# First FFN layer: weight rounding and squares moved to ScalarE, and the order of tile 0 changed

## What is computed

```python
def _quant_weight(w):
    gamma = jnp.mean(jnp.abs(w)) + EPS
    wq = jnp.clip(jnp.round(w / gamma), -1.0, 1.0) * gamma
    return w + jax.lax.stop_gradient(wq - w)
def _quant_act(x):
    scale = Q_MAX / jnp.clip(jnp.max(jnp.abs(x), axis=-1, keepdims=True), EPS)
    xq = jnp.clip(jnp.round(x * scale), -Q_MAX - 1.0, Q_MAX) / scale
    return x + jax.lax.stop_gradient(xq - x)
def bitlinear(x, w):
    return jnp.einsum('bsi,oi->bso', _quant_act(x), _quant_weight(w))
h = bitlinear(x, w1)
h = jnp.square(jax.nn.relu(h))
return bitlinear(h, w2)
```

## Time and profile before

| | us |
|---|---|
| median of 3 runs | 1647.94 (1645.99 to 1648.37) |
| the profiled execution | 1649.19 |
| its span, first to last instruction | 1647.9 |
| busy: PE, DVE, ACT, POOL | 1518.6, 1232.9, 888.3, 690.4 |
| share of the span: PE, DVE, ACT, POOL | 92%, 75%, 54%, 42% |
| mean granted TensorE clock | 0.975 |

### The profile page before, as it was taken

How to read it: one execution, slowest core, us unless ns; L and a number is a source line. 1 busy time by engine, 2 the same in 40 slices (tenths; PEclk the granted TensorE clock), 3 DMA queues, 4 the chain that set the end, 5 groups by cost and what they waited for, 6 DMA issues and landing times.

```text
span 1647.9 us, 26508 instructions
## 1 busy us (share of the span) xinstructions
PE 1518.6 (92%) x8800; PEld 1188.3 (72%) x8842; DVE 1232.9 (75%) x3031; ACT 888.3 (54%) x2404; POOL 690.4 (42%) x832
## 2 busy tenths in 40 slices
PE   4899999999999999999998789999986799999987
PEld 4778888888888888888886556666655576666653
DVE  4777776777777767767778867777787878888774
ACT  3666665666656656566666233333323366666655
POOL 2445555465555546455555000000004455555443
PEclk8999999999999999999998899999999799999999
DMA  6011111111110111111345666666655001111000
GB/s 263 14 42 62 40 65 39 39 65 48 50 58 39 65 40 52 52 49 54 123 174 191 223 221 207 219 210 216 219 194 182 14 20 52 46 52 40 26 14 26
DMA packets 50823, 156.71 MB, mean 95 GB/s; under 512 B 5888, under 2 KB 6016, under 8 KB 49280
## 3 DMA queue, kind: packets, MB, share of 16 engines
q1 hardware_dynamic: 50688, 155.02, 26.5%
HBM read 113.05 MB, written 41.94 MB: 94 GB/s over the span
## 4 chain that ended last, share of the span: by engine, by line
PE 66%; DVE 21%; ACT 5%; issue 5%; DMA 1%; POOL 1%; SPq 0%; DVEq 0%; ACTq 0%; POOLq 0%
PE bank L287 10%; PE bank L317 9%; PE bank L370 9%; PE bank L1140 8%; PE quad L357 5%; PE bank L1194 3%; PE quad L1169 3%; PE quad L345 3%; PE quad L347 3%; PE quad L346 3%; DVE bh L2015 2%; DVE wk L1971 2%; PE bank L329 2%; PE quad L1670 2%; PE bank L1578 2%
## 5 line engine op out<-in xcount | busy, mean ns | idle before, releaser
L535 ACT ACTIVATE Pt<-Pt,small 128x384 f32<-128x384 f32 (+1 forms) x256 | 172.8, 682 | 118.7 <-DVE small L754 118.5
L317 PE MATMUL bank<-wq,xT 128*128 128x512 f32 x768 | 207.1, 405 | 3.9 <-DVE wq L649 3.3
L370 PE MATMUL bank<-PT,vv 128*128 128x512 f32 x672 | 201.2, 408 | 9.2 <-DVE PT L739 5.4
L961 POOL TENSOR_SCALAR Pt<-Pt,small 128x384 f32<-128x384 f32 (+1 forms) x256 | 162.5, 648 | 86.9 <-DVE small L762 86.7
L754 DVE CUSTOM_DVE_ANT_0 Pt<-quad,mask,small 128x384 f32<-128x384 f32 (+1 forms) x256 | 171.2, 679 | 28.2 <-PE quad L347 26.8
L1140 PE MATMUL bank<-wq,ot 128*128 128x512 f32 x768 | 190.1, 400 | 1.6 <-DVE xr L1286 0.8
L739 DVE TENSOR_TENSOR PT<-quad,PT 128x512 fp32r<-128x512 f32 x224 | 153.7, 686 | 40.4 <-ACT PT L527 39.7
L1140 PEld LDWEIGHTS bank<-wq,ot 128*128 128x128 f32 x768 | 143.2, 190 | 34.2 <-issue 3.6
L317 PEld LDWEIGHTS bank<-wq,xT 128*128 128x128 f32 x768 | 137.9, 190 | 30.7 <-DVE wq L649 4.6
L949 POOL TENSOR_TENSOR t<-t 128x512 f32<-128x512 f32 x64 | 84.0, 1313 | 151.4 <-DVE t L720 151.4
L370 PEld LDWEIGHTS bank<-PT,vv 128*128 128x128 f32 x672 | 117.7, 191 | 32.7 <-DVE PT L739 13.7
(11 more groups left out here) (269 smaller groups left out, 3533.5 us busy)
## 6 DMA issues: line engine op xcount, KB each, us to landing
ot_scratch<-OT SPq DMA_DIRECT2D x64, 512.0 KB, 2.7
ot<-ot_scratch SPq DMA_DIRECT2D x64, 512.0 KB, 3.8
wkv_f<-in_w SPq DMA_DIRECT2D x12, 512.0 KB, 5.6
wkc_f<-in_w SPq DMA_DIRECT2D x12, 512.0 KB, 6.7
wkv_f<-in_wg SPq DMA_DIRECT2D x11, 512.0 KB, 4.7
wkv_f<-in_wd SPq DMA_DIRECT2D x11, 512.0 KB, 5.3
wkv_f<-in_wu SPq DMA_DIRECT2D x10, 512.0 KB, 4.7
stg<-in_ctxT SPq DMA_DIRECT2D x16, 256.0 KB, 3.3
```

The source lines that it names most:

```text
L317: ins = pe.matmul(bQ[:], xT[p][:, k, qt * 128:qt * 128 + 128], wq[j][:, g, k, :], start=(part == 0 and k == 0), stop=(part == 2 and k == 3))
L370: ins = pe.matmul(bO[:], vv[x][:, bg % 2, kt, :], PT[y][:, k % 2, :], start=(kt == 0 and n == 0), stop=(kt == tiles_in(i) - 1 and n == 2))
L535: act.activation(p, p, ACT.Exp, bias=nm[:, i % 2, h:h + 1], scale=-1.0, accum_out=sm[:, i % 2, h:h + 1]).then_inc(f["s_exp"], 1)
L961: pool.tensor_scalar(p, p, ri[:, i % 2, h:h + 1], 1.0, ALU.mult, ALU.mult).then_inc(f["p_n"], 1)
```

## The change

Four things are changed, all in the first FFN layer.

1. Ternary chunks: w1's last two, w2's last six and the second layer's T steps of tiles up to 13 are no longer compared by DVE. ACT multiplies the raw chunk by 1/gamma and adds 12582912 in f32, which rounds to whole numbers, in place (`act_levels`, first pass); a second pass subtracts it and writes bf16; DVE clips to -1 and +1 (`dve_clip`). The new semaphore t_lev counts the passes, and the raw buffer is free behind the second. `dve_gamma` and `dve_l_scale` work out one reciprocal more.
2. Squares: ACT squares each half of the relu in place with the scale inside the operation (`act_square`); DVE only rounds. The chain of small operations for the scale takes a maximum with the root of the bound and one operation less stands ahead of the scale.
3. Order: `pe_w2_sum` and `dve_gamma(1)` come ahead of group 3 of tile 0; w2's last two chunks come behind the squares on ACT; the loads of steps 0 to 2 come ahead of the ot loads 13 and 14, and ACT takes these three magnitudes at the end of tile 0 and not in tile 1.
4. The load of rope signals on the semaphore of the constants, and waits for the first use of these.

```diff
+WHOLE = 12582912.0
...
-        sp.dma_start(rope[:], a["rope"]).then_inc(f["tables_in"], 16)
+        sp.wait_ge(f["consts"], 1)
+        sp.dma_start(rope[:], a["rope"]).then_inc(f["const"], 16)
...
+    both = [k for k in range(ends[NT - 2]) if seq[k][0] == "T"]
...
+            elif k - 3 in both:
+                sp.wait_ge(f["t_lev"], 2 * (mem["shared"] + done[k - 3]))
...
             sp_ot(4 * n + 12)
+            if n < NT - 2:
+                sp_w(range(3) if n == 0 else range(ends[n + 1], ends[n + 2]))
             if n == 0:
                 sp_ot(13)
                 sp_ot(14)
-            if n < NT - 2:
-                sp_w(range(3) if n == 0 else range(ends[n + 1], ends[n + 2]))
...
+        pe_w2_sum()
         pe_y(0, 3)
-        pe_w2_sum()
         pe_y(1, 0)
...
+    def act_l(k):
+
+        if seq[k][0] == "A":
+            act_l_abs(k)
+        else:
+            w = seq[k][1]
+            act.wait_ge(f[f"g_w{k % 3}"], 16 * (k // 3 + 1))
+            act.wait_ge(f["w_gamma"], 2 * (2 + w) + 2)
+            mem["act_levels"](chunk(k), wraw[k % 3], gam1[:, w, 4:5], mem["shared"] + both.index(k))
+
+    def act_w2(q):
+        act.wait_ge(f[f"f_in{(0, 1, 3, 6)[q // 2]}"], (96, 96, 32, 32)[q // 2])
+        mem["act_ternary"](1, q)
+
+    def act_square(n, j):
+        s = slice(j * 1024, j * 1024 + 1024)
+        act.wait_ge(f["u_max"], 5 * n + 5)
+        act.wait_ge(f["relu"], 6 * n + 2 * j + 2)
+        act.activation(r_[:, s], r_[:, s], ACT.Square, scale=cl[:, n % 2, 22:23]).then_inc(f["relu"], 1)
...
     def act_program():
+        act.wait_ge(f["w_gamma"], 2)
+        mem["act_ternary"](0, 6)
+        mem["act_ternary"](0, 7)
+        act.wait_ge(f["w_gamma"], 4)
+        act_w2(2)
         for n in range(NT):
             act_xq(n)
+            if n == 0:
+                act_w2(3)
+                act_w2(4)
+                act_w2(5)
...
-            if n == 1:
-                act_l_abs(0)
-                act_l_abs(1)
+            for j in range(2):
+                act_square(n, j)
+            if n == 0:
+                act_w2(6)
+                act_w2(7)
             for j in range(2):
                 act_hT(n, j)
-            for k in visits(n, "A")[2 if n == 1 else 0:]:
-                act_l_abs(k)
+            if n < NT - 2:
+                for k in range(3) if n == 0 else range(max(ends[n], 3), ends[n + 1]):
+                    act_l(k)
...
+            dve.reciprocal(gm[:, 4:5], gm[:, 0:1]).then_inc(f["w_gamma"], 1)
...
         v.settle()
-        v.did(dve.scalar_tensor_tensor(c[:, 19:20], c[:, 17:18], c[:, 17:18], eps, ALU.mult, ALU.max))
-        v.settle()
-        v.did(dve.reciprocal(c[:, 20:21], c[:, 19:20]))
-        v.settle()
-        v.did(dve.tensor_tensor(c[:, 22:23], c[:, 20:21], c[:, 21:22], ALU.mult))
+        v.did(dve.tensor_scalar(c[:, 18:19], c[:, 17:18], float(1e-5 ** 0.5), None, ALU.max))
+        v.settle()
+        v.did(dve.reciprocal(c[:, 20:21], c[:, 18:19]))
+        v.settle()
+        dve.tensor_scalar(c[:, 22:23], c[:, 20:21], float(127 ** 0.5), c[:, 16:17],
+                          ALU.mult, ALU.mult).then_inc(f["u_max"], 1)
+        v.did(dve.tensor_tensor(c[:, 19:20], c[:, 18:19], c[:, 18:19], ALU.mult))
+        v.settle()
         v.did(dve.tensor_scalar(c[:, 23:24], c[:, 19:20], 1.0 / 127, gam[:, 1, 0:1], ALU.mult, ALU.mult))
...
-        dve.wait_ge(f["relu"], 4 * n + 2 * j + 2)
-        v.did(dve.scalar_tensor_tensor(r_[:, s], r_[:, s], col(n)[:, 22:23], r_[:, s], ALU.mult, ALU.mult))
-        v.settle()
+        dve.wait_ge(f["relu"], 6 * n + 5 + j)
         after(dve, f["ht"], 2 * (n - 1) + j + 1)
         dve.tensor_scalar(hh[:, s], r_[:, s], MAGIC, None, ALU.add).then_inc(f["hh"], 1)
...
-        v.did(dve.memset(eps, 1e-5))
-        dve_norm(0)
-        mem["dve_ternary"](0, 6)
-        mem["dve_ternary"](0, 7)
         dve.wait_ge(f["w_sum"], 2)
         mem["dve_gamma"](1, bM[:, 0:8])
-        for q in range(3):
-            dve_w2(q)
-        dve_w2(3)
-        dve_w2(4)
+        mem["dve_ternary_clip"](0, 6)
+        dve_norm(0)
+        mem["dve_ternary_clip"](0, 7)
+        mem["dve_ternary_clip"](1, 2)
+        dve_w2(0)
+        dve_w2(1)
...
+            if n == 0:
+                for q in (3, 4, 5):
+                    mem["dve_ternary_clip"](1, q)
             dve_hh(n, 0)
             dve_hh(n, 1)
...
-                for q in range(5, 8):
-                    dve_w2(q)
+                for q in (6, 7):
+                    mem["dve_ternary_clip"](1, q)
             dve_x2(n)
             if n < NT - 2:
                 for k in visits(n, "T"):
-                    dve_l(k)
+                    mem["dve_clip"](chunk(k), mem["shared"] + both.index(k))
...
+            dve.reciprocal(g[:, 4:5], g[:, 0:1]).then_inc(f["w_gamma"], 1)
+
+        def act_levels(out, r, inv, k):
+
+            act = nc.scalar
+            act.activation(r, r, ACT.Copy, bias=WHOLE, scale=inv).then_inc(f["t_lev"], 1)
+            act.wait_ge(f["t_lev"], 2 * k + 1)
+            act.activation(out, r, ACT.Copy, bias=-WHOLE).then_inc(f["t_lev"], 1)
+
+        def dve_clip(out, k):
+
+            nc.vector.wait_ge(f["t_lev"], 2 * k + 2)
+            nc.vector.tensor_scalar(out, out, -1.0, 1.0, ALU.max, ALU.min).then_inc(f["w_ter"], 1)
...
+        shared = [(0, 6), (0, 7)] + [(1, q) for q in range(2, 8)]
+
+        def act_ternary(w, q):
+            k = shared.index((w, q))
+            act_levels(ternary(w, q), mem["w2_raw"][q], gm[:, w, 4:5], k)
+
+        def dve_ternary_clip(w, q):
+            dve_clip(ternary(w, q), shared.index((w, q)))
```

More of the change, by code:

```diff
@@ L886, in dve_program @@
         dve_v_lo(0)
-        dve.wait_ge(f["tables_in"], 16)
+        dve.wait_ge(f["const"], 64)
         for qt in range(2):
@@ L1035, in col @@
         return cl[:, n % 2, :]
-    eps = mem["small"][:, 89:90]
     seq = [("A", 0, c) for c in range(8)]
@@ L1166, in pe_up @@
                 l1["pe_xa_turn"](1)
-            after(pe, f["relu"], 4 * (n - 1) + j + 1)
+            after(pe, f["relu"], 6 * (n - 1) + j + 1)
             for k in range(4):
@@ L1241, in act_relu @@
     def act_relu(n, j):
-        act.wait_ge(f["u_max"], 4 * n + j + 1)
+        act.wait_ge(f["u_max"], 5 * n + j + 1)
         after(act, f["hh"], 2 * (n - 1) + j // 2 + 1)
@@ L1304, in dve_norm @@
         v.did(dve.tensor_scalar(c[:, 16:17], c[:, 11:12], gam[:, 0, 0:1], None, ALU.mult))
-        v.settle()
-        v.did(dve.scalar_tensor_tensor(c[:, 21:22], c[:, 16:17], 127.0, c[:, 16:17], ALU.mult, ALU.mult))
     def dve_l_scale(n):
@@ L1314, in dve_l_scale @@
             dve.tensor_reduce(gm[:, 3:4], bT[0][:, 0:8], AX, ALU.add).then_inc(f["w_gamma"], 1)
-            dve.wait_ge(f["w_gamma"], 2 + w + 1)
+            dve.wait_ge(f["w_gamma"], 2 * (2 + w) + 1)
             v.did(dve.tensor_scalar(gm[:, 0:1], gm[:, 3:4], 1.0 / (512 * 2048), 1e-5, ALU.mult, ALU.max))
@@ L1336, in dve_up @@
             dve.tensor_reduce(c[:, 24 + j:25 + j], quad[:, j, :], AX, ALU.max).then_inc(f["u_max"], 1)
-        dve.wait_ge(f["u_max"], 4 * n + 4)
+        dve.wait_ge(f["u_max"], 5 * n + 4)
         v.did(dve.tensor_reduce(c[:, 14:15], c[:, 24:28], AX, ALU.max))
@@ L2233 @@
 SEMAPHORES = """
-const consts v_step g_step tables_in mask_in tables stg0 stg1 x_first w_raw0 w_raw1 w_raw2 w_raw3 w_raw4 w_raw5 w_hi w_lo
+const consts v_step g_step mask_in tables stg0 stg1 x_first w_raw0 w_raw1 w_raw2 w_raw3 w_raw4 w_raw5 w_hi w_lo
 c_hi c_lo ln_var ln_rs ln_x xt_mm xt_hi xt_lo
@@ L2238 @@
 s_mm s_ev s_exp s_ri p_n pt_mm pt_hi pt_lo pv_mm o_hi o_lo ot0
-f_in0 f_in1 f_in2 f_in3 f_in4 f_in5 f_in6 w_abs w_sum w_gamma w_ter wo_lo
+f_in0 f_in1 f_in2 f_in3 f_in4 f_in5 f_in6 w_abs w_sum w_gamma t_lev w_ter wo_lo
 g_row0 g_row1 g_row2 g_ot0 g_ot1 g_ot2 g_ot3 g_w0 g_w1 g_w2 y_mm x1 x_var x_rs xh xt xq
@@ L2325, in dve_gamma @@
             dve.tensor_reduce(g[:, 3:4], sums, AX, ALU.add).then_inc(f["w_gamma"], 1)
-            dve.wait_ge(f["w_gamma"], w + 1)
+            dve.wait_ge(f["w_gamma"], 2 * w + 1)
             v.did(dve.tensor_scalar(g[:, 0:1], g[:, 3:4], 1.0 / (512 * 2048), 1e-5, ALU.mult, ALU.add))
@@ L2331, in dve_gamma, with ternary @@
             v.settle()
+            dve.reciprocal(g[:, 4:5], g[:, 0:1]).then_inc(f["w_gamma"], 1)
[7 more added lines that the diff above has]
+            nc.vector.tensor_scalar(out, out, -1.0, 1.0, ALU.max, ALU.min).then_inc(f["w_ter"], 1)
+        def ternary(w, q):
+            return mem[("w1", "w2")[w]][q // 2][:, q % 2 * 1024:q % 2 * 1024 + 1024]
+        shared = [(0, 6), (0, 7)] + [(1, q) for q in range(2, 8)]
[4 more added lines that the diff above has]
+            dve_clip(ternary(w, q), shared.index((w, q)))
         def dve_ternary(w, q):
             dve, v, g = nc.vector, mem["v"], gm[:, w, :]
-            out3 = mem[("w1", "w2")[w]][q // 2][:, q % 2 * 1024:q % 2 * 1024 + 1024]
+            out3 = ternary(w, q)
             r = mem["w2_raw"][q]
@@ L2341, in block_kernel @@
```

(2 more changed lines are left out.)

## The result

The changed kernel takes **1628.4 us** (median of 4 runs, 1626.82 to 1630.63) where the kernel before takes 1647.84 on the same chip: a ratio of 0.9885, 95% interval 0.9868 to 0.9902, or 19.4 us less. The profiled execution took 1627.65 us with a span of 1626.4 and a mean granted clock of 0.981.

A forecast was written before the change was run, and what follows sets the result against it. It took PE to bound the regular tiles, with time lost in tiles 0 and 1 and at the change to the second layer. 10.4 + 1.1 + 0.45 + 2.6 - 0.2 = 14.35 us off 1647.94 gave 1633.6 us, range 1630.0 to 1640.0.

The forecast's parts named there:

- In the regular tiles nothing that VectorE or ScalarE gives up can shorten anything: First FFN layer, tiles 2 to 13: PE is fully busy, so no gain except tile 8's wait, 0.45 us.
- The prediction's own sign: First FFN layer: the regular tiles keep their length; no size beyond the 0.45 us for tile 8's wait.
- Head of tile 0: Column sum of w2 magnitudes ahead of group 3 of tile 0's y product: 2.05 us lost on the path.
- Rival (a): PE's clock falls in the new wait at 914 us: two y groups cost 4.6 us, 1638.2 in all; chance 0.15.
- Tile 0: PE's 7.11 us wait for hh goes; down product starts at 945.7 instead of 956.11 us: 10.4 us gained.
- rival (b): The first chunks land late and hold xq of tile 1 on ACT: 2.9 us, 1636.5 in all; chance 0.08.
- Prices: ACT passes 1.145 and 0.97 us, a chunk 2.2, squares 1.15 each; a DVE clip 0.35 us.
- Tile 1: From its up product to the next group 0, 9.2 instead of 10.28 us: 1.1 us gained.
- Up 14 to up 15: End of the layer: rows and aq come sooner, last up product starts at 1233.85 instead of 1236.45: 2.6 us gained.
- rival (d): End of layer: aq early by ring order, gain 4.0 us, total 1632.2, or 1631.5 with tile 15's clock held; chance 0.11.
- Behind up 15: In tile 15 the squares stand behind qT on ACT: about 0.2 us lost.

The follow-up runs named there:

- the sum behind: The changed kernel with the small column sum of w2 back behind group 3 of tile 0's y product, its scale made inside tile 0's norm: 1630.9 us, ratio 0.9888.

## Why the prediction was right and wrong, by its steps

**"In the regular tiles nothing that VectorE or ScalarE gives up can shorten anything": wrong, and the largest miss.** 4.50 us came from there, 0.45 foreseen. The seven kernels with the squares on ScalarE have 231.8 us from up 2 to up 14, the three without 235.9 to 236.3. The step took PE as the only bound, since no bracket in PE's timeline showed a wait and 232.48 of 235 us were busy. Numbers against it were there: 2.5 us not busy, PEld's eleven waits for hh, and the path of 10.28 us in tile 1. DVE writes the second half of hh 9.54 us behind the up product (1186.45 - 1176.91); PE wants it at 8.93 + 0.51 = 9.44. The prediction shortened that path for tile 1 and never laid it beside the regular tiles; it worked out there what the change leads to (hh at 8.6 us, covered), not what stood before. The later chunks are worth 0.35 us there with the squares on VectorE (236.27 against 235.92), near the 0.45 foreseen for tile 8, and 0.02 with them on ScalarE (231.79 against 231.77). The prediction's own sign, that the regular tiles keep their length, failed too. With the 4.05 us that this term lacked the sum would have given 1629.6, by that alone below the range; the table puts 3.5 us more in other terms.

**Head of tile 0: right, one risk sized too low.** 1.72 us of waiting and 0.25 of product are 1.97 us, 2.05 foreseen. Rival (a), the clock falling in that wait, was given 0.15. It came in three of four profiles with that order, and cost 1.4 to 1.6 us in each, not 4.6: only group 3 ran slow. In the changed kernel's own profile it did not come; its other executions have no trace, so whether it came there is not shown.

**Tile 0: the mechanism right, the closeness in part luck.** hh's halves end at 935.56 and 936.60 us (935.5 and 936.6 foreseen), group 0 of tile 2 starts at 937.44 (937.2), the down product at 945.70 (945.7). But the head of this execution began 0.95 us later than before's, which hides that the stretch came out that much shorter than the sum: to up 1 it gained 10.85 us with 0.28 given back to rival (b), so 11.1 against 10.4. With tile 0's chunks back on VectorE the gain is lost. With the sum behind, rival (b) took 1.4 us more.

**Prices.** A pair of passes 1.14 and 1.06 us (1.145 and 0.97 foreseen), a chunk in 2.1 us (2.2), two squares 2.21 (2.3). A clip takes 0.43 us, where half of a pass over f32, 0.35, was taken; nothing hung on it. The Trainium skill, page "VectorE: DVE Perf Modes", section "Side-by-side: where the cycles go for N=2048 bf16", counts four values a cycle in its fastest mode and 158 cycles fixed at 0.96 GHz; for 1024 values that is an estimate of 0.43 us, and this trace agrees with 0.43.

**Tile 1: right.** 1.13 us, 1.1 foreseen.

**Up 14 to up 15: mechanism right, the term mis-sized.** 3.75 us, 2.6 foreseen. The rows were asked for at 1199.80 us and held nothing any more; aq came 1214.62 - 1209.88 = 4.7 us after its issue, where 5.9 was taken. This is nearly rival (d), but aq was still last, by little: xq of tile 15 starts at 1216.52 us right behind the conversion of aq, while xh would have let it start 0.43 us behind the transposes (as in the run with the squares back), at 1216.34. The 4.0 us of that rival isn't what the prediction's own time for xh gives, 1235.15 - 1231.65 = 3.5. The Trainium skill, page "DMA: Bandwidth & Descriptors", section "Anatomy of one DMA", has a fit for loads that GpSimd issues; its estimate of 4.4 us for 1 MB was nearer than the row of another load, though SP issued this one. The runs put both cases side by side: 4.7 to 5.2 us with the rows asked for 10 us ahead, 5.8 and 5.9 with them 4.9 us ahead. The 7.8 us of before lie outside both; why is left open.

**Behind up 15: the size and the sign.** The squares behind qT cost 0.67 us (16.57 against 15.91 and 15.90 us in the two runs with the squares on VectorE), 0.2 foreseen. But with the wait ahead of tile 15 short (0.78 us for xh instead of 3.29), PE's clock held. Tile 15's up and down products before, and the up product after, in tables of stages:

```profile
1236.00:1240.00 4.00, 4.00 (x19) 2.00 (x18) 2.35 (x4) 1.78 (x4) 4.00 (x3) 0.77 0.56 217
1248.00:1252.00 4.00, 3.75 (x16) 2.02 (x18) 2.51 (x3) 2.05 (x3) 1.34 (x2) 0.57 0.00 0
```
```profile
1217.00:1221.00 4.00, 3.83 (x20) 1.95 (x20) 2.07 (x4) 2.26 (x5) 4.00 (x2) 1.00 0.73 288
```

This is worth 18.26 - 15.90 = 2.4 us (0.7 of it up to the first product with aq, 1.7 from the hh transposes to the second), and appears in every run in which the rows come early, except in that with the sum behind, whose down product ran slow (18.13). Rival (d) had 0.7 of it.

## What to carry to other kernels

A timeline that joins like instructions can hide a wait inside a row; compare a row's length with the same work elsewhere, and read the rows of PEld beside those of PE, before calling an engine the only bound. Where two paths of a loop are within a few tenths of each other, shortening the one that looks covered pays once per turn of the loop. Work that waits for a transfer must not stand ahead of work that the critical engine waits for: three small magnitudes in front of xq ate all of a 5 us gain.
